# Two PSUM rings, six banks: four for maxima and two for exponentials instead of three and three

## The reference

```
Q, K, V = split_heads(x_flat @ Wq + bq), ... Wk ..., ... Wv ...
attn = softmax(einsum('bhnd,bhmd->bhnm', Q, K) * scale, axis=-1)
out  = einsum('bhnm,bhmd->bhnd', attn, V) @ Wo + bo
y    = layernorm(out + x_flat) * gamma + beta
```

## Time and profile before

| | us |
|---|---|
| median of 3 runs | 5567.02 (5562.84 to 5569.83) |
| the profiled execution | 5566.89 |
| its span, first to last instruction | 5565.1 |
| of it the first layer, about | 0 to 3750 |
| a slot without additions | 26.96 |

### The profile page before, as it was taken

One profiled execution on the slowest core, in us unless ns is written; L12 is line 12 of the kernel. 1 busy time (PEld: TensorE's weight loads), 2 busy tenths in 40 slices (PEclk: granted clock), 3 DMA queues, 4 the chain that ended last, 5 costly groups with the idle time before them and its releaser, 6 DMA issues. The chain is left out here.

```text
span 5565.1 us, 80727 instructions
## 1 busy us (share of the span) xinstructions
PE 5272.6 (95%) x25104; PEld 2415.7 (43%) x25104; DVE 4856.9 (87%) x7060; ACT 3871.3 (70%) x7513; POOL 4792.9 (86%) x3309
## 2 busy tenths in 40 slices
PE   7999999999999999999999999996888898898888
PEld 3444444444444444444444444432333333333333
DVE  6888888888888888888888888855999999999998
ACT  3666666666666666666666666665777778787786
POOL 4888887888888788888778888874999999999998
PEclk8999999999999999999999999997999999999999
DMA  4111121211112211111120110127889888888887
GB/s 141 37 54 46 41 63 61 69 50 39 52 39 67 82 44 50 37 54 54 60 69 18 33 34 18 48 69 188 234 232 235 227 230 236 228 237 232 231 232 203
DMA packets 377806, 608.37 MB, mean 109 GB/s; under 512 B 87424, under 2 KB 110976, under 8 KB 375936
## 3 DMA queue, kind: packets, MB, share of 16 engines
q1 hardware_dynamic: 367872, 585.91, 37.8%
q10 hardware_dynamic: 9504, 17.31, 1.5%
HBM read 457.04 MB, written 127.14 MB: 105 GB/s over the span
## 5 line engine op out<-in xcount | busy, mean ns | idle before, releaser
L649 DVE TENSOR_REDUCE mpart<-ps 128x1 f32<-128x512 f32 x4096 | 2539.3, 682 | 532.9 <-PE ps L406 532.2
L533 ACT ACTIVATE exps<-ps 128x512 f32<-128x512 f32 x4096 | 2146.5, 601 | 1138.1 <-PE ps L413 1111.5
L406 PE MATMUL ps<-k_st,q_ring 96*128 96x512 f32 x4096 | 1776.8, 435 | 18.0 <-DMA k_st<-qk_split 13.5
L413 PE MATMUL ps<-q_ring,k_st 98*128 98x512 f32 x4096 | 1621.2, 397 | 4.0 <-ACT exps L533 3.6
L1368 POOL TENSOR_TENSOR hc<-hh,c_rep 128x1024 f32<-128x1024 f32 x512 | 1206.8, 2374 | 118.7 <-DVE hh L1326 88.1
L622 POOL TENSOR_TENSOR held<-exps 128x512 f32<-128x512 f32 x768 | 987.7, 1311 | 359.9 <-ACT exps L533 359.9
L406 PEld LDWEIGHTS ps<-k_st,q_ring 96*128 96x128 f32 x4096 | 774.3, 189 | 1132.7 <-DVE mpart L649 696.2
L622 POOL TENSOR_TENSOR sums<-exps 128x512 f32<-128x512 f32 x896 | 1132.5, 1280 | 70.3 <-ACT exps L533 68.2
L424 PE MATMUL ps<-exps,v_ring 128*32 128x512 f32 x8192 | 1091.0, 605 | 0.0
L1326 DVE TENSOR_TENSOR_SCAN hh<-d_a,carry,ps 128x512 f32<-128x512 f32 x864 | 1077.8, 1266 | 0.0
L413 PEld LDWEIGHTS ps<-q_ring,k_st 98*128 98x128 f32 x4096 | 778.2, 190 | 137.9 <-ACT exps L533 19.0
(11 more groups left out here) (116 smaller groups left out, 4397.0 us busy)
## 6 DMA issues: line engine op xcount, KB each, us to landing
d_a<-dt_dram SPq DMA_DIRECT2D x1040, 256.0 KB, 4.4
su<-u_dram SPq DMA_DIRECT2D x160, 256.0 KB, 4.6
qk_split<-hilo SPq DMA_DIRECT2D x128, 256.0 KB, 2.3
out_dram<-out_sb SPq DMA_DIRECT2D x128, 256.0 KB, 2.0
heads_in<-out_dram SPq DMA_DIRECT2D x32, 1024.0 KB, 5.3
q_ring<-qk_split SPq DMA_DIRECT2D x384, 64.0 KB, 2.0
k_st<-qk_split SPq DMA_DIRECT2D x45, 512.0 KB, 7.3
dt_dram<-dt SPq DMA_DIRECT2D x33, 512.0 KB, 4.4
```

Source lines behind the costliest of these rows:

```text
L406: nc.tensor.matmul(d_bank(("max", m, t)), q_ring[0:PARTS, m % 4, 128 * i:128 * i + 128], k_st[0:PARTS, g % 2, chunk(kc)], start=True, stop ...
L413: nc.tensor.matmul(a_bank(("exp", n, t)), k_st[0:SHIFT, n // NCH % 2, 128 * t:128 * t + 128], q_ring[0:SHIFT, n % 4, :], start=True, stop= ...
L533: nc.scalar.activation(exps[:, u % EXPS, CH * half:CH * half + CH], a_bank(("exp", n, t)), ACT.Exp, scale=SCALE).then_inc(a_done, 1)
L649: nc.vector.tensor_reduce(mpart[:, m % 2, t % 4, t // 4:t // 4 + 1], d_bank(("max", m, t)), AX.X, ALU.max).then_inc(d_done, 1)
```

## The change

Of the six banks, VectorE's ring gets four (banks 0 to 3) and ScalarE's ring two (banks 4 and 5). The two waits follow: an entry of ring d waits for entry k-4, an entry of ring a for entry k-2. Nothing else is touched: the same instructions in the same order on every engine, and the same transfers.

```diff
-        MAX_BANK, EXP_BANK, OUT_BANK, DEN_BANK = 0, 3, 6, 7
+        MAX_BANK, EXP_BANK, OUT_BANK, DEN_BANK = 0, 4, 6, 7
...
         def d_bank(key):
-            return ps[:, MAX_BANK + d_at[key] % 3, :]
+            return ps[:, MAX_BANK + d_at[key] % 4, :]

         def a_bank(key):
-            return ps[:, EXP_BANK + a_at[key] % 3, :]
+            return ps[:, EXP_BANK + a_at[key] % 2, :]
...
                 def d_room(key):
-                    if d_at[key] >= 3:
-                        pe.wait_ge(d_done, d_at[key] - 2)
+                    if d_at[key] >= 4:
+                        pe.wait_ge(d_done, d_at[key] - 3)

                 def a_room(key):
-                    if a_at[key] >= 3:
-                        pe.wait_ge(a_done, a_at[key] - 2)
+                    if a_at[key] >= 2:
+                        pe.wait_ge(a_done, a_at[key] - 1)
```

## The result

The changed kernel takes 5818.68 us (median of 4 runs, 5814.80 to 5866.61) against 5567.92 for the kernel before: 4.5% slower, ratio 1.0473 with a 95% interval of 1.0453 to 1.0493. The forecast was 5817, in a range of 5775 to 5857. One of the four runs, at 5866.61 us and without a trace, had a mean granted clock of 0.937 where the others had 0.980 to 0.983, and pulls the ratio up; the medians give 5818.68 / 5567.92 = 1.0450. The profiled execution took 5820.18 us.

The account below looks back on a forecast made before the run. TensorE was taken to set the first layer's pace. Plain slots 197, other entries 31, caught-up rounds 17 and slots 126 and 127 4 made 249, say 250 us, on 5567.02: 5817 us, range 5775 to 5857.

Parts of the forecast that it names:

- The round: One undisturbed round, counted from M0: E2 and E3 loads wait for E0's and E1's exponentials, lengthening it 3.06 to 3.33 us.
- The hand-over of 0.05 us: From the end of an exponential to the weight load waiting for its bank, read in slot 126: 0.05 us.
- the late load's 0.34: Behind M3's late weight load, E3 starts 0.34 us later, since no earlier matmul covers the load.
- the 0.42: From E3's late start to AV: 0.42 us.
- The plain slot: A slot without additions: eight rounds together 1.54 us longer, +197 us over 128 slots.
- Other entries and the rounds that had caught up: Non-E entries in ScalarE's ring wait for E2, +31 us; 88 rounds where VectorE catches up pay 0.27, +17 us.
- VectorE's ring of four: Removes M3's waits in rounds 4 to 7, 0.66 us per slot, already netted; can bring no more.
- rival 1: E2 does not in fact wait and only M3's waits go: 67 us faster, 5500 us; 2%.
- rival 2: VectorE's wait stays beside ScalarE's, so rounds 4 to 7 pay 0.27 in full: 5879 us; 4%.
- Rival 3: New pauses in every round bring TensorE's clock down at times: about 300 us more, 6115 us; 2%.

Follow-up runs that it names:

- the last pair of runs: Denominators' sums moved to the end of round 1 of the next slot: three banks each, 5577.38 us; four for maxima and three for exponentials, 5494.98 us.
- the second control: Kernel before with all denominators' sums at the end of round 1 of the next slot, three banks per ring, one idle: 5577.38 us, ratio 1.0019.
- the mirror image: Kernel before with two banks for maxima and four for exponentials: 6026.13 us, ratio 1.0828.

## Why the prediction was right

By its steps:

- *The round.* E2's load was put at +1.42, M3 at +1.76, E3's load at +1.90, AV at +2.32, the next M0 at +3.33. The trace has 1.42, 1.76, 1.91, 2.34 and 3.33 to 3.34. The hand-over of 0.05 us, taken from slot 126, holds for E2 and E3 in all 992 rounds of slots 1 to 124, and the late load's 0.34 with them (0.34 to 0.39); the 0.42 measures 0.43.
- *The plain slot.* From the starts of the maximum tiles, the median over 71 plain slots goes from 26.98 to 28.50 us: +1.52. The prediction wrote 1.54, but that is a slip of its sum: 4 x 0.27 + 0.20 + 3 x 0.08 is 1.52, which makes 195 us of its 197 and 247 of its 249. Undisturbed rounds gain 0.26 to 0.27, round 4 0.20, rounds 5 to 7 0.08 each, as said.
- *Other entries and the rounds that had caught up.* A projecting slot goes from 29.71 to 32.01 (median of 24), +2.30 where the steps give 1.52 + 0.43 + 0.27 + 0.19 = 2.41; a finishing slot from 31.42 to 33.77 (27), +2.35 where they give 1.52 + 0.27 + 0.19 + 2 x 0.19 = 2.36. Inside these there are errors of both signs. The second projection's round is 4.66 as worked out. The first one's and the variance's are 4.72 instead of 4.66, the spread's 4.72 instead of 4.62. Round 6 was said to pay 0.08 and pays nothing (4.19 and 4.20 in a finishing slot): it had more of M's wait to lose than the plain rounds it was taken from. Round 7 was said to pay 0.27 in both kinds and pays 0.21 to 0.22.
- *VectorE's ring of four.* Worth nothing at this round, as said: with three banks the time is the same. M3's gap was real, and a bank there is worth 82 us where ScalarE keeps its third; the price of taking it from ScalarE's ring was larger. The Trainium skill's rule on recurring gaps (Perfetto Trace Analysis, Optimization Strategy) thus agrees with the last pair of runs; what a bank costs the ring that it is taken from, which decided the change, it does not say.
- *The rivals.* E2 does wait (rival 1), and no round with held sums of a plain slot is above 3.34 (rival 2). Rival 3 came in small: two waits in every round left the granted clock at 1.00, but behind the third wait of a round it fell five times, and its sign, a clock below 1.00 in the first layer, is there. The Trainium skill (TensorE: Matmul & The Clock Gate, A second HAM failure mode: psum-queue depth-cycling) tells of a clock that goes up and down as TensorE idles shortly between groups of matmuls; the five stretches at 0.50, 31 us in all, agree with it, and the other rounds do not show it.
- *What the clock cost.* Slots 60 and 93 last 35.32 and 35.33 us where the median is 33.77. In the run with M3 ahead of E2 slots 125 and 126 stayed at 1.00; there they last 33.45 and 31.87 us, here 34.99 and 34.46. In slot 127 the clock fell in both runs; its rounds 4 to 6 last 17.51 us here, and those of slot 126 at 1.00, in the other run, 12.41. That makes 1.6 + 1.6 + 1.5 + 2.6 + 5.1, an estimate of 12 us.

The sum was 249 us and the spans differ by 253.2. That they agree so closely is luck in part. The prediction had the clock at nothing, and of the 253 us some 241 are left for the waits when the estimated 12 are taken off, against 247 by its terms rightly added; about 4 of the missing 6 are in the projecting slots. The mechanism holds, and the 241 us of the waits alone, a time of 5808, lie in the forecast's range as well.

## What to carry to other kernels

Price a ring of buffers by one round: the reader's end two (or three) entries back plus the hand-over, against the time at which the writer's fixed order wants that buffer; whatever stands behind the waiting instruction moves with it. Look at the granted clock by stretches as well, since a mean that rounds to 1.00 can hide short falls. A gap on one ring says what a buffer there would be worth, and not what it costs on the ring it is taken from; look for a third place to take it. And where a ring must be short, reordering the writer so that its first entries go early gives back most of the loss.

## What the runs showed that was not expected

- Gathering work in one place can cost time though the work is the same: with the sixteen passes of the denominators at the end of round 0 the kernel takes 37 us more than with them split in two, since there they wait for GpSimd's last pair sum, and 10 us more with them at the end of round 1.
- The fourth bank, where it was free, brought 82 us and not 67. A finishing slot, counted with a gain of 0.66 - 0.38 = 0.28 us, goes from 31.70 to 31.21 (medians of 27). Its round 6 alone goes from 4.19 to 3.93, so its rounds had more of M's waits than the plain rounds they were taken from.
- The granted clock has one weak place in this layer. Wherever a profiled run of this case shows 0.50 between 100 us and its last exponential tile, the stretch starts 0.8 to 1.6 us behind a spread of the denominators: five times in the changed kernel and in the one without the fourth bank, twice with M3 ahead of E2, twice with E0 and E1 first, twice in the second control, once in the mirror image, never in the other four. The wait of that load does not decide it alone: with E0 and E1 first it is 0.57 us too, and the clock behind all 29 spreads ahead of slot 126 stays at 1.00.
